# Other slots for W_down's mixes, splits and evictions, and another order inside a slot, beside the first FFN block

## The reference, cut to what matters

```python
h = rms_norm(rms_norm(emb[x]) @ proj.T)
n = layernorm(h)
q, k, v = n @ Wq.T, n @ Wk.T, n @ Wv.T            # 16 heads of 32
q, k = layer_norm(q*gamma+beta) * 32**-0.5, layer_norm(k*gamma+beta)
attn = where(causal, (q @ k.T)**2, 0)
h = h + (attn @ v / (attn.sum(-1) + eps)) @ Wo.T
x = fwht(layernorm(h) * SU_ug) / 64
x = silu(x @ W_gate.T * Ws_g * 64) * (x @ W_up.T * Ws_u * 64)   # 512 -> 2048
x = fwht(x * SU_dp) / 64
h = h + x @ W_down.T * (Ws_dp * 64)                             # 2048 -> 512
```

## Time and profile before

| | us |
|---|---|
| median of 3 runs (1349.68 to 1355.08) | 1351.8 |
| the profiled execution | 1351.9 |
| its span, first to last instruction | 1350.0 |

### The profile page before, as it was taken

How to read it: one execution, slowest core, us unless ns; L and a number is a source line. 1 busy time by engine, 2 the same in 40 slices (tenths; PEclk the granted TensorE clock), 3 DMA queues, 4 the chain that set the end, 5 groups by cost and what they waited for, 6 DMA issues and landing times.

```text
span 1350.0 us, 18434 instructions
## 1 busy us (share of the span) xinstructions
PE 1236.2 (92%) x7065; PEld 591.2 (44%) x7065; DVE 646.8 (48%) x1136; ACT 418.5 (31%) x731; POOL 568.2 (42%) x487
## 2 busy tenths in 40 slices
PE   6765787677999999999999999999999999999999
PEld 3452333233444444444444444444444444444444
DVE  2668457654465355536354545544553555361110
ACT  4663675251143213321233023311331133211210
POOL 0552265522176416642475237531764166411210
PEclk9887788788999999999999999999999999999999
DMA  9800033272353244523452344424533345120000
GB/s 330 320 1 1 16 71 71 47 133 55 96 112 83 63 95 103 109 48 94 109 110 56 86 100 108 73 71 99 104 79 71 86 112 99 21 76 14 1 1 32
DMA packets 231043, 113.17 MB, mean 84 GB/s; under 512 B 209412, under 2 KB 210744, under 8 KB 230456
## 3 DMA queue, kind: packets, MB, share of 16 engines
q1 hardware_dynamic: 219776, 77.78, 26.4%
q0 software_dynamic: 10240, 33.56, 8.4%
q10 hardware_dynamic: 952, 0.75, 0.2%
HBM read 53.08 MB, written 9.70 MB: 46 GB/s over the span
## 4 chain that ended last, share of the span: by engine, by line
PE 73%; DVE 7%; DMA 6%; ACT 4%; issue 4%; POOL 4%; SPq 0%; DVEq 0%; ACTq 0%; POOLq 0%
PE bank L1357 22%; PE bank L1358 22%; PE bank L1359 22%; PE bank L1515 3%; DMA prod<-sg 3%; DMA wgu<-h 1%; POOL h L509 1%; POOL hid L565 1%; DMA wd<-h 1%; ACT wgu L1099 1%; DMA xT<-in_L_tok_proj_weight 1%; PE bank L1552 1%; PE bank L1350 1%; ACT xT L1099 1%; DVE xT L910 1%
## 5 line engine op out<-in xcount | busy, mean ns | idle before, releaser
L1357 PE MATMUL bank<-xT,wgu 128*128 128x512 f16 x1024 | 391.3, 382 | 1.4 <-DVE xT L910 1.4
L1358 PE MATMUL bank<-xT,wgu 128*128 128x512 f16 x1024 | 391.3, 382 | 0.0
L1359 PE MATMUL bank<-xT,wgu 128*128 128x512 f16 x1024 | 390.8, 382 | 0.0
L565 POOL TENSOR_TENSOR hid<-a,hid 128x512 f16<-128x512 f32 x128 | 176.4, 1378 | 261.8 <-ACT hid L1099 261.4
L994 DVE SCALAR_TENSOR_TENSOR a<-bank,kap,sg 128x512 f32<-128x512 f32 x128 | 96.0, 750 | 335.7 <-PE bank L1359 291.3
L1357 PE MATMUL bank<-wd,hid 128*128 128x512 f16 x512 | 195.2, 381 | 0.0
L1358 PE MATMUL bank<-wd,hid 128*128 128x512 f16 x512 | 195.0, 381 | 0.0
L1359 PE MATMUL bank<-wd,hid 128*128 128x512 f16 x512 | 195.0, 381 | 0.0
L1359 PEld LDWEIGHTS bank<-xT,wgu 128*128 128x128 f16 x1024 | 100.8, 98 | 122.9 <-issue 3.6
L1357 PEld LDWEIGHTS bank<-xT,wgu 128*128 128x128 f16 x1024 | 101.0, 99 | 121.8 <-issue 3.9
L1358 PEld LDWEIGHTS bank<-xT,wgu 128*128 128x128 f16 x1024 | 100.8, 98 | 119.1 <-issue 3.3
(11 more groups left out here) (203 smaller groups left out, 1398.6 us busy)
## 6 DMA issues: line engine op xcount, KB each, us to landing
out<-a SPq DMA_DIRECT2D x24, 256.0 KB, 2.2
wgu<-in_L_ffn_W_gate SPq DMA_DIRECT2D x4, 1024.0 KB, 15.4
wgu<-in_L_ffn_W_up SPq DMA_DIRECT2D x4, 1024.0 KB, 15.5
wd<-in_L_ffn_W_down SPq DMA_DIRECT2D x4, 1024.0 KB, 15.3
out<-h_row SPq DMA_DIRECT2D x8, 256.0 KB, 2.0
hid<-att_table,ids_p POOLq DMA_INDIRECT x72, 3.5
xT<-in_L_tok_proj_weight SPq DMA_DIRECT2D x1, 1024.0 KB, 10.3
p<-in_L_attn_Wq SPq DMA_DIRECT2D x1, 1024.0 KB, 13.0
```

The source lines that it names most:

```text
L565: nc.gpsimd.tensor_tensor(hid[:, 1, s, :], a32[:, :], hid[:, 0, s, :], ALU.subtract)\
L1357: mm(dst, w[0], v[0], start=first, stop=False)
L1358: mm(dst, w[0], v[1], start=False, stop=False)
L1359: return mm(dst, w[1], v[0], start=False, stop=final)
```

## The change

The table of squares becomes (4,3,3,2,2,2) per slot. The mixes move to slots 1 to 10 instead of 2 to 12, with two in slots 3, 5 and 7. The splits start in slot 9 as before, but then come two per slot; the first four Hadamard products come in slots 11, 12, 13, 14 instead of 10, 11, 12, 14. `fit_scale` is parted: `split_scale` (slot 8) makes only what the splits need, the rest follows in slot 9, and ACT's splits wait for `split_scaled` instead of `bound_done`. In a slot, ACT's order becomes evictions, silu, heads, `p<-prod`, `hid<-a`, units, splits; DVE's `prod`, evictions, heads, `a`, scales, mixes, splits; POOL's heads, `p` low, `hid` low, units low. The halves of block 1's heads (`head_rows`, `head_high`, `head_low`, `o_turn`) come one slot after PE's sums. POOL's fetch of `h_row` waits until `oT` has landed, instead of until PE has made the first rows by Wo; this last edit holds for all blocks.

```diff
-DOWN_SQUARES = (3, 3, 3, 3, 2, 2)
+DOWN_SQUARES = (4, 3, 3, 2, 2, 2)
-MIX_BESIDE = (2, 3, 4, 5, 6, 7, 8, 8, 9, 10, 11, 12)
-SPLIT_BESIDE = (9, 10, 11, 13, 13, 13, 14, 14, 14, 15, 15, 15, 16, 16, 17, 18)
-HADA_BESIDE = (10, 11, 12, 14, 15, 16, 16, 17, 17, 18, 18, 19, 19, 20, 21, 22)
+MIX_BESIDE = (1, 2, 3, 3, 4, 5, 5, 6, 7, 7, 9, 10)
+SPLIT_BESIDE = (9, 10, 10, 11, 11, 12, 12, 13, 13, 14, 14, 15, 15, 16, 16, 17)
+HADA_BESIDE = (11, 12, 13, 14, 15, 16, 16, 17, 17, 18, 18, 19, 19, 20, 21, 22)
@@ SP, first_block
-                    if s in SUMS_AT:
-                        o_turn(1, SUMS_AT.index(s))
-                for s in (16, 17, 18):
-                    last_unit_turns(s)
+                    if s - 1 in SUMS_AT:
+                        o_turn(1, SUMS_AT.index(s - 1))
+                last_unit_turns(16)
+                o_turn(1, 3)
+                last_unit_turns(17)
@@ POOL
-                    pool.wait_ge(S["wo_ready"], 4 * n + 1)
+                    pool.wait_ge(S["oT_land"], 16 * QUADS * n)
...
                 fetch(1, s)
+                if s - 1 in SUMS_AT:
+                    head_low(1, SUMS_AT.index(s - 1))
+                product(1, s)
                 feed(0, s)
                 for x in units_beside(s):
                     unit_low(x)
-                product(1, s)
@@ DVE
+            def split_scale():
                 dve.wait_ge(S["bound_pow"], 3)
                 link(power_of_two(gl[:, 8:9], red[:, 10:11]))
+                nc.vector.tensor_scalar(wsd_s[:, :], ws_d, gl[:, 8:9], 2.0 ** 13, ALU.mult, ALU.mult).then_inc(S["split_scaled"], 1)
...
-                feed(0, s, UP0[s] if s < FT else None)
                 for v in down_hadas(s - 1):
                     down_unit(v)
-                for v in down_splits(s):
-                    unit_low(UNITS + v)
+                if s - 1 in SUMS_AT:
+                    head_rows(1, SUMS_AT.index(s - 1))
+                feed(0, s, UP0[s] if s < FT else None)
...
                 if s == FIT_BESIDE + 2:
+                    split_scale()
+                if s == FIT_BESIDE + 3:
                     fit_scale()
                 for k, at in enumerate(MIX_BESIDE):
                     if at == s:
                         down_mix(MIXED_BEFORE + k)
+                for v in down_splits(s):
+                    unit_low(UNITS + v)
@@ ACT
-                    act.wait_ge(S["bound_done"], 1)
+                    act.wait_ge(S["split_scaled"], 1)
...
+                for v in down_hadas(s - 1):
+                    down_unit(v)
                 feed(0, s, GATE[s % 2])
+                if s - 1 in SUMS_AT:
+                    head_high(1, SUMS_AT.index(s - 1))
+                product(1, s)
+                feed_high(0, s)
                 for x in units_beside(s):
                     unit_high(x)
-                for v in down_hadas(s - 1):
-                    down_unit(v)
                 for v in down_splits(s):
                     unit_high(UNITS + v)
-                feed_high(0, s)
-                product(1, s)
```

More of the change, by code:

```diff
@@ L238, in tower @@
         gu_ss gu_rn gu_pow gu_scaled turned st_diag st_scaled st_hi st_lo st_low turn_land0 turn_land1 turn_land2
-        d_ss d_mix sc_ready bound_asked bound_sum bound_low bound_pow bound_done
+        d_ss d_mix sc_ready bound_asked bound_sum bound_low bound_pow bound_done split_scaled
         d_hada d_hi d_lo oT_land xn_land
@@ L539, in fetch, with head_low @@
                     gather(n + 1, 0, NEXT_AT.index(s))
+            def head_low(n, q):
+                pool.wait_ge(S["oh_done"], QUADS * n + q + 1)
+                nc.gpsimd.tensor_tensor(o16[:, 1, :], wide[:, :], o16[:, 0, :], ALU.subtract)\
+                    .then_inc(S["ol_done"], 1)
             def attend(n, s):
                 sums_at, wo_at = (O_AT0, ()) if first(n) else (SUMS_AT, WO_AT)
-                if s in sums_at:
-                    q = sums_at.index(s)
-                    pool.wait_ge(S["oh_done"], QUADS * n + q + 1)
-                    nc.gpsimd.tensor_tensor(o16[:, 1, :], wide[:, :], o16[:, 0, :], ALU.subtract)\
-                        .then_inc(S["ol_done"], 1)
+                if s in sums_at and n != 1:
+                    head_low(n, sums_at.index(s))
                 if s in ROWS_AT and not first(n):
@@ L714, in fit_terms, with fit_scale @@
                 nc.vector.reduce_sum(st4[:, 10:11], ssw[:, 0:4], AX.X).then_inc(S["bound_asked"], 1)
-            def fit_scale():
+            def split_scale():
                 dve.wait_ge(S["bound_pow"], 3)
                 link(power_of_two(gl[:, 8:9], red[:, 10:11]))
+                nc.vector.tensor_scalar(wsd_s[:, :], ws_d, gl[:, 8:9], 2.0 ** 13, ALU.mult, ALU.mult).then_inc(S["split_scaled"], 1)
+            def fit_scale():
                 link(nc.vector.tensor_tensor(gl[:, 12:13], gl[:, 6:7], gl[:, 7:8], ALU.min))
@@ L721, in fit_scale @@
                 link(nc.vector.tensor_scalar(s_w, gl[:, 13:15], gl[:, 12:13], None, ALU.mult))
-                link(nc.vector.tensor_scalar(wsd_s[:, :], ws_d, gl[:, 8:9], 2.0 ** 13, ALU.mult, ALU.mult))
                 link(nc.vector.tensor_scalar(s_w, s_w, 2.0 ** -4, None, ALU.mult))
@@ L948, in attend @@
             def attend(n, s):
-                if s in SUMS_AT:
+                if s in SUMS_AT and not by_matmul(n):
                     head_rows(n, SUMS_AT.index(s))
```

## The result

The changed kernel takes 1337.0 us (median of 4 runs, 1336.6 to 1337.9), beside 1353.0 for the kernel before in the same comparison (1349.7 to 1355.1): a ratio of 0.9885, 95% interval 0.9863 to 0.9907. So 15.9 us are gained; 30 were forecast, and the time lies just above the range's end of 1336. The profiled execution took 1337.1, its span 1335.3. Executions of one kernel often fall into two groups 3 to 5 us apart (the kernel before: near 1349.5 and near 1354), so two medians of four runs that differ by 1 or 2 us don't tell two kernels apart.

A forecast was written before the change was run, and what follows sets the result against it. PE's waits in the first FFN block were taken as the bound, behind an overfull ACT and DVE in slot 8. The legs summed to a gain of 29 to 34, taken as 30: 1351.9 less 30, so 1322, range 1312 to 1336.

The forecast's parts named there:

- leg 2: Bound sum in slot 7 on PE: comes at 202.2 to 204.3 against 204.07, taking back the gain at the heads of slot 4.
- leg 1: Heads of slot 4: start at about 181 instead of 186.52, without the slow clock after them, as POOL's low part comes sooner.
- a sum after 206: Sign against the forecast: the bound's sum of slot 7 reaching PE later than 206, where 202 to 205 was expected.
- Legs 4 and 5: Slots 12 to 15, then on to v11: gain 24 to 29 at the heads of slot 15, 29 to 34 at the end.
- leg 3: Heads of slot 8 to v0: waits of 5.58 and 12.52 go, slot 12 starts at 231.8 to 236.5, gain 19 to 24.
- Nothing is charged: Later blocks: the earlier fetch of `h_row` takes a place that PE's work covers, so no cost was counted.
- DVE becomes the bound: Rival, block 0's slots: twelve mixes at 4.3 instead of 2.9 us; gain 20, time 1332, range 1328 to 1340; chance 0.20.

## Why the prediction was off

**What failed is leg 2, together with a wait that leg 1 left out.** The prediction had the sum of slot 7 at 202.2 to 204.3, and named a sum after 206 as a sign of being wrong; it came at 211.15.

- *Slot 2.* Leg 1 went from silu to silu on ACT and never asked what PE itself wants in slot 2: `bound_sum(1)`, behind DVE's `half_terms(1)`, behind `a` of slot 1. Silu of slot 1 was foretold right (165.0; 164.82). PE was ready for that sum at 165.96 and `a` of slot 1 ended at 166.2, so with the eight operations at the 1.4 us of before a wait of nearly 2 us was there to be seen; the rest of the 5.32 came because they took 4.9 beside POOL. So PE fell behind: silu of slot 3 came 3.5 us later than forecast (182.07), the heads of slot 4 at 187.41 instead of 181, with no wait. The run with the terms in slot 0 shows the wait's cause; it is worth 3.4 us of the stretch at most, and 1.6 if the clock's part in slots 0 and 1 is taken off.
- *DVE's mixes.* Seven stand ahead of the sum, four before; the prediction's text counted five. It gave a mix 2.9 us where the seven took 3.4 on average (23.6 in all), and let them hold back only `a` of slots 4 and 6. But ACT's new order waits for `prod`, so a late DVE also delays the next silu: slot 4 lasted 10.2 us on ACT instead of 6.1. (The leg's own sum has a slip of 0.6: 178.6, 6.1 twice and 6.6 give 197.4, not 198.0.) Cutting the mixes brought the sum to 203.78 and the time to 1323.4.
- *Slot 11.* From the sum to slot 9's start it took 12.3 us, as forecast. From there to up of slot 11 it took 17.1, where the leg's times on the clock leave 13.8 to 16.3 (its terms, added up, give 12.8 to 18.0, so those bounds were too narrow). The wait for `a` of slot 10 was foreseen at up to 2.7 and is 3.12; not priced was the low clock behind it: 0.50, the 1.2 GHz level, for 5.0 us (240.60 to 245.60), 2.5 us lost. Slot 12 began at 246.84, not 231.8 to 236.5.

**Legs 4 and 5 held, and of leg 3 that v0's wait goes.** Heads of slot 15 come 8.64 us after the slot's start with a wait of 2.87 (forecast 8.6 and 3.0), v6 8.5 later (8.0), v11 15.1 after v6 (15.2) with a wait of 2.45 (2.6). The row sum follows its matmuls at once:

```profile
295.65 0.75 DVE L932 SCALAR_TENSOR_TENSOR h<-bank,gl,h_row 128x512 f32<-128x512 f32 x1 [4.35 <-PE bank L1372]
```

**"Nothing is charged" for the fetch in later blocks** was wrong by 2.0 us (985.1 to 987.1 behind the stretch). The prediction named it as a thing to look at, but did not price it.

So of the 15 us missing against the forecast's 1322, 13 are in the stretch (block 1's FFN at 348.16, not 335) and 2 behind it. The outcome is the rival "DVE becomes the bound" (1328 to 1340), with its mechanism, but not with its sum. It counted five mixes at 4.3 us ahead of the bound's sum, 21.5 us; seven at 3.4 made 23.6, two errors that nearly cancel. All twelve took 42.6 us, 3.55 each, near the middle between its 2.9 and 4.3: the second halves averaged 1.92 of at most 2.1 us, the first halves 1.62, so its objection, that POOL is idle in part of every slot, weighed about half. And it had neither the wait in slot 2 nor the 2 us behind the stretch. That 1337 lies in its range is in part luck. The rule under which that rival stood, in the Trainium skill, "SBUF — State Buffer", section "Who interferes with whom" (two SBUF inputs on VectorE against a GpSimd operation that reads SBUF, one waits for the whole of the other), agrees with the trace: those 8-column operations of DVE that ran long end with POOL's to 0.03 us, and with POOL only writing the units' low parts, the mixes fell by 7.3 us.

## What to carry to other kernels

Before a chain is moved, list every wait of the engine that counts between here and its goal, the small ones too: the 5.3 us hung on eight tiny operations, at their price beside a busy engine and not at their price alone. Where an engine's queue is short of slack up to a point, a wait lifted in one slot comes back in the next; only less work, or work put into an idle stretch, brings time. Before two traces are compared by a stretch, compare them where the code is the same: one execution here was up to 1.8 us ahead of another there. An edit that holds for all blocks is priced in the later ones too: 0.3 us in each of them took back a part of what it won once.

## What the runs showed of the hardware

- An operation of DVE on 8 columns takes 0.15 to 0.17 us, and beside POOL's `tensor_tensor` of 1.16 four of eight took 1.01 to 1.08 and ended when POOL's did: their price is the rest of POOL's operation, not their own size.
- Both sides pay: a mix half goes from 1.21 to 2.14, POOL's 128x512 subtraction from 1.16 to 2.14. In the whole stretch the same DVE instructions, in the same order, took 115.8 or 133.2 us by ACT's order alone.
- Mixes cut to 32 of 1024 columns still took 0.5 to 0.6 us each half on average.
- A low clock behind a wait costs only where PE is not about to wait again: with 0.80 from the heads of slot 15 to v6 that way took 8.55 us, with 1.00 it took 8.54; behind v6, 0.90 instead of 1.00 cost 1.7.
